# Slot sums of a mixture-of-experts layer: high and low part of an output in one product of 512 columns, four PSUM banks, halves added at the end

## The chip, the cores and the metric

The kernel runs on one core of a Trainium2 chip. The metric is the device time of one execution in microseconds; the kernel before took 657.53 us in the median of three runs (656.26 to 657.68). PE is TensorE, DVE VectorE, ACT ScalarE, POOL GpSimd and SP SyncE. PSUM, into which PE writes, has eight banks (`bank[0]` to `bank[7]`), each 512 fp32 columns on 128 partitions.

## The reference, cut to what matters

Eight sequences of 256 tokens of 256 values go through an expert layer, an attention layer and the same expert layer again:

```
x = x + 0.5 * moe(layernorm(x))
x = x + attention(layernorm(x))
x = x + 0.5 * moe(layernorm(x))

def moe(x):                      # 64 experts, 8 for each token, 32 slots for each expert, F = 96
    logits = x @ router_w.T
    wts, idx = top_k(softmax(logits), 8); wts = wts / sum(wts)
    # each expert takes its first 32 tokens, in order of position (position-major over the 8 sequences)
    h = silu(xg @ w1.T) * (xg @ v1.T)
    y = h @ w2
    return sum over the slots of a token of weight * y
```

## The kernel before, in words

An expert layer has three stages. The router computes logits, masks and, for each expert, the list of its tokens, and writes the normalised tokens to a table in HBM. Then 16 slot groups follow (`slot_step`, s = 0 to 16), each of 4 experts with 32 slots, 128 slots together. In step s PE transposes the gathered tokens of group s + 1 (L1173), adds the finished outputs of group s - 3 into the tokens (`sum_slots`, L1177), transposes `hidden` of group s - 1 (L1236), does the up products of group s (L1243) and the down products of group s - 1 (L1253). ACT copies the transposed tokens (`slotsT`, L560) and the transposed hidden values (`hiddenT`, L564), computes the gate (L570) and scales the down product to `y_parts[:, s, 0]`, the high part, rounded to fp32r (L574). DVE makes the one-hot marks (L852), the hidden values (L858) and the low part of the output (L865), which is the output less its high part. A sum product takes a one-hot matrix of 128 slots by 128 token columns as weights and `y_parts` as the moving operand, and so adds each slot's row to its token's row; high and low part are two products of 256 columns into the same place. Only the first 64 rows of each sequence (512 tokens) are summed in layer 0 (the others come into play when the last held token lies later), and 64 + 16 rows in layer 1, the 16 as "narrow" sums in `bank[5]` (L1185). The wide sums lie in `bank[6]` and `bank[7]`, each with four sequences: two on the partitions, two on the columns. Before the slots PE puts the tokens themselves there (`take_tokens`, L1212), so that the sum is the new x.

Other banks in the slot stage: `bank[0]` transposed tokens, `bank[1]` up products, `bank[2]` transposed hidden values, `bank[3]` down products, `bank[4]` slot numbers and last token. PE runs in program order, and each engine waits on semaphores; nothing but the order of the calls sets who comes first on an engine.

After layer 0 ACT copies the two banks to x in four copies (L685), DVE takes the statistics of the first tokens straight from `bank[6]` (L962), computes the moments (L806), normalises the first 512 tokens (L1040), and attention begins with nine projections (`first_fills`): two transposes xT, k, q, q, v, q, q, v. For each, ACT takes the high part out of PSUM (`take_high`) and DVE the low part (`take_low`). Between them ACT and DVE split the attention weights into high and low parts (`split_high`, `split_low`, L675 and L996); a projection waits until its weights are split (`split_by`). Weights arrive by DMA on SP's queue, the last of them `wo_raw`. `keep_busy` (L1205) gives PE products with no use in stretches where it would idle.

After layer 1 DVE copies the narrow sums to `stage` (L946), ACT `bank[6]` (L661), DVE `bank[7]` (L948), and six narrow and four wide stores go out on the queues of SP, POOL and ACT (L362, L366), each behind the semaphore `staged` of its part.

## Time and profile before

| | |
|---|---|
| median of 3 runs | 657.53 us (656.26 to 657.68) |
| profiled execution | 657.74 us, its span 655.9 us |
| layer 0's slot steps | about 38.4 to 85.4 us |
| attention | about 90.5 to 572 us |
| layer 1's slot steps | about 596.2 to 649.3 us |
| last stores issued | 652.7 us |

The span is the time from the first to the last instruction in the profile; the 1.8 us around it belong to the execution's own time. In rows of a timeline the first column is the start in us from the span's begin and the second how long the instruction, or the merged run of instructions, took. PEld rows are weight loads, which run beside the products. Ends of products on PE are modelled, so the distance between starts is the better measure. Brackets tell how long the engine was idle before the row, and for whom it waited.

### The profile page before, as it was taken

To read this page: it belongs to the slowest core of one execution; us is meant where nothing else is said; L and a number is where in the kernel's file an instruction comes from. 1 tells how busy PE (TensorE), PEld (TensorE's weight loads), DVE (VectorE), ACT (ScalarE), POOL (GpSimd) and SP (SyncE) were. 2 spreads that over 40 slices of the span, in tenths; PEclk is the share of its full clock that TensorE was granted. 3 is DMA by queue.
4 is the path that set the end of the run, shared out by engine and by line. 5 is a ranking of instruction groups with operands and counts; after the bars stand their busy time and mean duration, and the time that the engine had idled before them with its cause. 6 is when DMAs were issued, how large, how long until landed. Compare 5 with 4: busy or idle time off the path is not lost.

```text
span 655.9 us, 12187 instructions
## 1 busy us (share of the span) xinstructions
PE 623.6 (95%) x4572; PEld 536.4 (82%) x4572; DVE 504.9 (77%) x1316; ACT 386.0 (59%) x1048; POOL 52.2 (8%) x75
## 2 busy tenths in 40 slices
PE   8589989999999999999999999999999998997995
PEld 6367777999889999999889999989899997774774
DVE  6836668889997778889777788877788888694663
ACT  5724476677666655666665666656566665581442
POOL 3343000000000000000000000000000000034310
PEclk9779999999999999999999999999999999977998
DMA  8999870000000000000000000000000007175993
GB/s 315 338 412 418 307 263 1 2 1 1 0 1 1 1 1 1 0 1 1 1 1 1 1 0 1 1 1 1 1 0 1 1 11 311 36 270 182 420 397 105
DMA packets 27621, 62.53 MB, mean 95 GB/s; under 512 B 7014, under 2 KB 17382, under 8 KB 27558
## 3 DMA queue, kind: packets, MB, share of 16 engines
q1 hardware_dynamic: 25398, 55.97, 22.6%
q0 software_dynamic: 1664, 5.30, 2.1%
q8 instruction: 39, 0.64, 0.4%
q10 hardware_dynamic: 496, 0.43, 0.3%
q14 instruction: 24, 0.20, 0.1%
HBM read 54.34 MB, written 7.34 MB: 94 GB/s over the span
## 4 chain that ended last, share of the span: by engine, by line
PE 77%; DVE 10%; DMA 7%; ACT 2%; issue 1%; SPq 1%; POOL 0%; another core or an unknown queue 0%; POOLq 0%; DVEq 0%
PE bank L1401 19%; PE bank L1403 19%; PE bank L1402 19%; PE bank L1457 8%; PE bank L1243 3%; PE bank L1201 3%; DMA wo_raw<-wo_in 2%; DMA down_r<-down_in 2%; PE bank L1253 2%; PE bank L1173 1%; DMA slots<-token_table,slot_index 1%; DMA x<-x_in 1%; DVE probsT_lo L1101 1%; DVE negmax L1066 1%; DVE ln L806 1%
## 5 line engine op out<-in xcount | busy, mean ns | idle before, releaser
L718 ACT ACTIVATE probs<-bank,negmax 128x256 f32<-128x256 f32 x256 | 121.4, 494 | 0.7 <-DVE negmax L1066 0.6
L726 ACT CAST probsT_hi<-bank 128x512 fp32r<-128x512 f32 x128 | 68.7, 590 | 71.0 <-PE bank L1457 71.0
L701 ACT ACTIVATE o_hi<-bank,bv 128x512 fp32r<-128x512 f32 x64 | 44.2, 690 | 66.7 <-PE bank L1403 66.7
L1101 DVE TENSOR_TENSOR probsT_lo<-bank,probsT_hi 128x512 fp32r<-128x512 f32 x128 | 81.8, 680 | 0.5 <-ACT probsT_hi L726 0.5
L1066 DVE TENSOR_REDUCE negmax<-bank 128x2 f32<-128x512 f32 x128 | 81.7, 680 | 0.0
L1074 DVE TENSOR_SCALAR probs<-probs,rowinv 128x256 f32<-128x256 f32 x256 | 73.1, 349 | 2.3
L1401 PE MATMUL bank<-wo_hi,o_hi 128*128 128x256 f32 x256 | 73.1, 285 | 0.0
L1403 PE MATMUL bank<-wo_hi,o_lo 128*128 128x256 f32 x256 | 72.6, 284 | 0.0
L1403 PE MATMUL bank<-k_hi,q_lo 128*128 128x256 f32 x256 | 72.4, 283 | 0.0
L1402 PE MATMUL bank<-k_lo,q_hi 128*128 128x256 f32 x256 | 72.4, 283 | 0.0
L1402 PE MATMUL bank<-wo_lo,o_hi 128*128 128x256 f32 x256 | 72.3, 282 | 0.0
L1401 PE MATMUL bank<-k_hi,q_hi 128*128 128x256 f32 x256 | 72.2, 282 | 0.0
L1052 DVE SCALAR_TENSOR_TENSOR o_lo<-bank,bv,o_hi 128x512 fp32r<-128x512 f32 x64 | 48.0, 750 | 28.7 <-ACT o_hi L701 28.7
L1052 DVE SCALAR_TENSOR_TENSOR q_lo<-bank,bq,q_hi 128x512 fp32r<-128x512 f32 x64 | 47.9, 748 | 25.5 <-ACT q_hi L701 25.3
L1457 PE MATMUL bank<-ident,probs 128*128 128x128 f32 x512 | 66.4, 273 | 0.7 <-DVE probs L1074 0.7
L1457 PEld LDWEIGHTS bank<-ident,probs 128*128 128x128 f32 x512 | 57.3, 140 | 1.1 <-DVE probs L1074 1.1
L718 ACT ACTIVATION_READ_ACCUMULATOR probs<-bank,negmax 128x1 f32 x256 | 57.7, 226 | 0.0
L1401 PE MATMUL bank<-xT_hi,wq_hi 128*128 128x512 f32 x128 | 54.4, 425 | 1.0 <-DVE k_lo L1052 1.0
L1401 PE MATMUL bank<-probsT_hi,v_hi 128*128 128x512 f32 x128 | 51.1, 399 | 3.1 <-DVE probsT_lo L1101 2.9
L701 ACT ACTIVATE q_hi<-bank,bq 128x512 fp32r<-128x512 f32 x64 | 45.0, 703 | 12.5 <-PE bank L1403 12.5
L1401 PEld LDWEIGHTS bank<-k_hi,q_hi 128*128 128x128 f32 x256 | 48.8, 191 | 2.8 <-DVE q_lo L1052 0.3
L1402 PEld LDWEIGHTS bank<-k_lo,q_hi 128*128 128x128 f32 x256 | 48.8, 191 | 2.4
(181 smaller groups left out, 1342.7 us busy)
## 6 DMA issues: line engine op xcount, KB each, us to landing
up_r<-up_in SPq DMA_DIRECT2D x16, 768.0 KB
down_r<-down_in SPq DMA_DIRECT2D x14, 512.0 KB
up_q<-up_in SPq DMA_DIRECT2D x8, 768.0 KB, 8.8
up_o<-up_in SPq DMA_DIRECT2D x6, 768.0 KB
down_q<-down_in SPq DMA_DIRECT2D x8, 512.0 KB, 9.6
token_table<-xn SPq DMA_DIRECT2D x16, 256.0 KB, 2.4
down_o<-down_in SPq DMA_DIRECT2D x6, 512.0 KB
x<-x_in SPq DMA_DIRECT2D x4, 512.0 KB, 5.6
```

What stands on the lines that cost most here:

```text
L701: nc.scalar.activation(dst, src, ACT.Identity, bias=bias).then_inc(work_high, 1)
L718: nc.scalar.activation(probs[:, n % 2, t, :], scores_ps[head][:, qt * S:qt * S + S], ACT.Exp, bias=negmax[:, n % 2, t:t + 1], accum_out=ro ...
L726: nc.scalar.copy(probsT[0][:, head].rearrange("p c s -> p (c s)"), probsT_ps[head][:]).then_inc(probsT_high, 1)
L1052: nc.vector.scalar_tensor_tensor(lo, src, bias, hi.bitcast(f32), ALU.add, ALU.subtract).then_inc(work_taken, 1)
L1066: nc.vector.reduce_max(negmax[:, n % 2, 2 * head:2 * head + 2], scores_ps[head][:].rearrange("p (t s) -> p t s", t=2), AX.X, negate=True). ...
L1074: last = nc.vector.tensor_scalar(probs[:, n % 2, t, :], probs[:, n % 2, t, :], rowinv[:, n % 2, t:t + 1], None, ALU.mult)
L1101: nc.vector.tensor_tensor(probsT[1][:, head].rearrange("p c s -> p (c s)"), probsT_ps[head][:], probsT[0][:, head].rearrange("p c s -> p ( ...
L1201: last = mm(banks[n][:, D * pair:D * pair + D], marks[:, c:c + P], parts, start=start and pair == 0, stop=stop, skip_group_check=True)
L1401: mm(dst, w[0], m[0], start=start, stop=False, skip_group_check=shared)
L1402: mm(dst, w[0], m[1], start=False, stop=False, skip_group_check=shared)
L1403: return mm(dst, w[1], m[0], start=False, stop=stop, skip_group_check=shared)
L1457: last = nc.tensor.transpose(probsT_ps[head][:, c * S + qt * P:c * S + qt * P + P], probs[:, n % 2, 2 * head + qt, c * P:c * P + P], ident[:])
```

## The change

`sum_slots` issues one product of 512 columns where it issued two of 256: the moving operand is high and low part side by side. The high sums come to the first 256 columns of a bank and the low sums to the last 256. A bank then holds two sequences and not four, so that the wide sums take four banks (`wide_ps` = banks 2, 3, 6, 7), and the narrow ones all 512 columns of bank 5. The tokens go into the high halves, with `start=True` (banks 2 and 3 last, after the logits in them were copied). At the end ACT copies the high half to `stage` and DVE adds the low half to it, for each of the four banks and for the narrow one; the result goes to x after layer 0 and stays in `stage` after layer 1.

The banks freed for this: transposed hidden values move from bank 2 to free columns of bank 0, down products from bank 3 to bank 4. PE therefore waits for ACT's copy of the transposed tokens before it transposes `hidden`, and in step 1 for `limit_ready` before the down products. After layer 0 one `finish_tokens` stands ahead of the statistics, which are now taken from x, one behind the normalisation, and two behind the first two fills. The splits of weights on ACT are placed anew among the fills, and `keep_busy` after layer 0's sums has 16 products for 20.

```diff
-        def wide_sums(banks, b):
-            return banks[b // 4][WIDE * (b % 2):WIDE * (b % 2) + WIDE, D * (b // 2 % 2):D * (b // 2 % 2) + D]
+        wide_ps, narrow_ps, down_ps, idle_ps = bank[2:4] + bank[6:8], bank[5], bank[4], bank[1]
+        def pair_rows(b, low=0):
+            return wide_ps[b // 2][WIDE * (b % 2):WIDE * (b % 2) + WIDE, D * low:D * low + D]
...
-        def rows_of_bank(n, odd, count=4):
-            first = 4 * n + odd
-            return x[0:WIDE, 2 * first:2 * (first + count - 1):4, :]
+        narrow_stage = stage[:, 2, 0:D]
+        def stage_of(n):
+            return stage[:, n // 2, D * (n % 2):D * (n % 2) + D]
...
                     nc.scalar.copy(hiddenT[:],
-                                   bank[2][0:F, 0:P]).then_inc(hiddenT_ready, 1)
+                                   bank[0][0:F, KD * P:KD * P + P]).then_inc(hiddenT_ready, 1)
                 if layer == 0 and s == GROUPS:
...
                     act.wait_ge(down_done, down_seen.add())
-                    nc.scalar.activation(y_parts[:, s - 1, 0, :], bank[3][:, 0:D],
+                    nc.scalar.activation(y_parts[:, s - 1, 0, :], down_ps[:, 0:D],
                                          ACT.Identity, scale=slot_weight[:, s - 1:s]).then_inc(y_high, 1)
...
                 if layer == 1:
-                    act.wait_ge(bank_summed, 2 + 2)
-                    nc.scalar.copy(stage[:, 0, :], bank[6][:]).then_inc(staged[0], 1)
-                    act.wait_ge(staged[0], 1)
+                    copy_high_sums(PAIRS, narrow_stage, narrow_ps)
+                    for n in range(PAIRS):
+                        copy_high_sums(PAIRS + 1 + n, stage_of(n), wide_ps[n])
+                    act.wait_ge(staged[0], 2)
                     for odd in range(2):
                         store_wide(nc.scalar, 0, odd)
-                    act.wait_ge(staged[1], 1)
+                    act.wait_ge(staged[1], 2)
                     store_wide(nc.scalar, 1, 1)
...
+            def copy_high_sums(seen, dst, sums):
+                act.wait_ge(bank_summed, seen + 1)
+                nc.scalar.copy(dst, sums[:, 0:D]).then_inc(high_copied, 1)
             def split_high(n):
...
             expert_layer(0)
-            for n in range(2, 5):
+            for n in range(2, 4):
                 split_high(n)
             act.wait_ge(small_loaded, 64)
-            for n, seen in ((1, (bank_summed, 2)), (0, (first_sums_read, 1))):
-                act.wait_ge(*seen)
-                for odd in range(2):
-                    nc.scalar.copy(rows_of_bank(n, odd), bank[6 + n][WIDE * odd:WIDE * odd + WIDE, :].rearrange(
-                        "p (b d) -> p b d", b=2)).then_inc(x_final, 1)
-            split_high(5)
+            for n in range(PAIRS):
+                copy_high_sums(n, stage_of(n), wide_ps[n])
+            for n in range(4, 6):
+                split_high(n)
...
             warm(ACT.Exp)
-            for n in range(6, 8):
-                split_high(n)
             act.wait_ge(bq_scaled, 1)
             for n, job in enumerate(first_fills):
+                if n == 5:
+                    act.wait_ge(x_final, PAIRS)
                 take_fill(*job)
-                if 1 <= n < 5:
-                    split_high(n + 7)
+                if 1 <= n < 6:
+                    split_high(n + 5)
+                if n == len(first_fills) - 1:
+                    split_high(11)
                 if n >= SCORES_AT and n < SCORES_AT + 2:
...
                 else:
-                    dve.wait_ge(bank_summed, 2 + 1)
-                    nc.vector.tensor_copy(stage[:, 2, 0:D], bank[5][:, 0:D]).then_inc(staged[2], 1)
-                    dve.wait_ge(bank_summed, 2 + 3)
-                    nc.vector.tensor_copy(stage[:, 1, :], bank[7][:]).then_inc(staged[1], 1)
+                    add_low_sums(PAIRS, narrow_stage, narrow_ps, staged[2])
+                    for n in range(PAIRS):
+                        add_low_sums(PAIRS + 1 + n, stage_of(n), wide_ps[n], staged[n // 2])
...
                 with nc.vector.If(most >= FIRST[layer]):
-                    dve.wait_ge(bank_summed, (2, 5)[layer])
+                    dve.wait_ge(bank_summed, (PAIRS, 2 * PAIRS + 1)[layer])
                     for r in range(1, RANGES):
...
-                    last.then_inc(first_sums_read, 1)
-                    dve.wait_ge(first_sums_read, 1)
+                        last = nc.vector.bn_stats(stats[0:WIDE, 2 * odd, :], x[0:WIDE, 2 * odd, :])
+                    tie(last)
+            def add_low_sums(seen, dst, sums, done):
+                dve.wait_ge(high_copied, seen + 1)
+                nc.vector.tensor_tensor(dst, dst, sums[:, D:2 * D], ALU.add).then_inc(done, 1)
+            def finish_tokens(n):
+                dve.wait_ge(high_copied, n + 1)
+                for odd in range(2):
+                    rows = slice(WIDE * odd, WIDE * odd + WIDE)
+                    last = nc.vector.tensor_tensor(x[0:WIDE, 2 * (2 * n + odd), :], stage_of(n)[rows, :], wide_ps[n][rows, D:2 * D], ALU.add)
+                last.then_inc(x_final, 1)
...
             dve.wait_ge(bo_ready, 1)
-            dve.wait_ge(x_final, 4)
             normalise_tokens(0)
+            finish_tokens(1)
             for n, job in enumerate(first_fills):
...
                     normalise_probs(0)
+                if n < 2:
+                    finish_tokens(n + 2)
                 for m in in_fill.get(n, []):
                     split_low(m)
+            dve.wait_ge(x_final, PAIRS)
             step(0)
...
                 marks = onehot[:, s % MARKS, :]
+                parts = y_parts[:, s, :, :].rearrange("p l d -> p (l d)")
                 if layer == 1:
-                    for low in range(2):
-                        last = mm(bank[5][:, 0:D], marks[:, RANGE:FIRST[1]], y_parts[:, s, low, :], start=False,
-                                  stop=final and low == 1, skip_group_check=True)
+                    last = mm(narrow_ps[:], marks[:, RANGE:FIRST[1]], parts, start=False, stop=final, skip_group_check=True)
                     if final:
                         last.then_inc(bank_summed, 1)
-                for n in range(2):
-                    for low in range(2):
-                        last = sum_wide(bank[6:8], n, marks, y_parts[:, s, low, :], False, final and low == 1)
+                for n in range(PAIRS):
+                    last = mm(wide_ps[n][:], marks[:, n * P:n * P + P], parts, start=False, stop=final, skip_group_check=True)
                     if final:
...
-            def take_tokens():
-                for b in range(B):
-                    mm(wide_sums(bank[6:8], b), ident[:, 0:WIDE], x[:, 2 * b, :], start=b % 4 < 2, stop=False,
+            def take_tokens(layer):
+                for b in (4, 5, 6, 7, 0, 1, 2, 3):
+                    if b == 0:
+                        pe.wait_ge(logits_ready, 4 * layer + 4)
+                    mm(pair_rows(b), ident[:, 0:WIDE], x[:, 2 * b, :], start=True, stop=False,
                        skip_group_check=True, tile_position=(0, WIDE * (b % 2)))
...
                 for b in range(B):
-                    mm(bank[5][:, 0:D], rows_into_place(b), x[WIDE:WIDE + NARROW, 2 * b, :], start=b == 0, stop=False,
+                    mm(narrow_ps[:, 0:D], rows_into_place(b), x[WIDE:WIDE + NARROW, 2 * b, :], start=b == 0, stop=False,
                        skip_group_check=True)
...
                 if s > 0:
+                    if s + 1 < GROUPS:
+                        pe.wait_ge(slotsT_ready, sT_seen.now() + 1)
                     pe.wait_ge(hidden_ready, hidden_seen.add())
-                    nc.tensor.transpose(bank[2][0:F, 0:P], hidden[:],
+                    nc.tensor.transpose(bank[0][0:F, KD * P:KD * P + P], hidden[:],
                                         ident[:]).then_inc(hiddenT_raw, 1)
...
                     pe.wait_ge(down_free, free_seen.add())
+                    if s == 1:
+                        pe.wait_ge(limit_ready, layer + 1)
                     for j in range(EG):
-                        last = mm(bank[3][32 * j:32 * j + 32, 0:D],
+                        last = mm(down_ps[32 * j:32 * j + 32, 0:D],
                                   hiddenT[:, 32 * j:32 * j + 32],
...
                 if layer == 0:
-                    keep_busy(20)
+                    keep_busy(16)
                 pe.wait_ge(limit_ready, layer + 1)
...
                 project(*job)
+            pe.wait_ge(x_final, PAIRS)
             step(0)
-            pe.wait_ge(x_final, 4)
             for i in range(BLOCKS - 1):
```

## Rows read from the trace of the kernel before

**Rows 1.** Page, part 1: busy us (share of the span) xinstructions of each engine.
```profile
PE 623.6 (95%) x4572; PEld 536.4 (82%) x4572; DVE 504.9 (77%) x1316; ACT 386.0 (59%) x1048; POOL 52.2 (8%) x75
```

**Rows 2.** Timeline, one slot step of layer 0: start, duration, engine, line, operands.
```profile
62.57 0.44 PE L1173 MATMUL bank<-ident,slots 128*128 128x128 f32 x2
...
62.74 1.01 PEld L1201 LDWEIGHTS bank<-y_parts,onehot 128*128 128x128 f32 x8
...
62.77 0.47 ACT L574 ACTIVATE y_parts<-bank,slot_weight 128x256 fp32r<-128x256 f32 x1 [0.24 <-PE bank L1253]
...
63.14 0.36 ACT L560 COPY slotsT<-bank 128x256 f32<-128x256 f32 x1
...
63.69 0.12 PEld L1236 LDWEIGHTS bank<-ident,hidden 128*96 128x96 f32 x1
...
65.22 0.44 PE L1173 MATMUL bank<-ident,slots 128*128 128x128 f32 x2
```

**Rows 3.** Timeline, the same point in two steps of layer 1.
```profile
629.87 0.44 PE L1173 MATMUL bank<-ident,slots 128*128 128x128 f32 x2
...
632.75 0.44 PE L1173 MATMUL bank<-ident,slots 128*128 128x128 f32 x2
```

**Rows 4.** Timeline, a projection: first and last of five 512-column products in a row.
```profile
97.02 0.39 PE L1402 MATMUL bank<-xT_lo,wq_hi 128*128 128x512 f32 x1
...
97.94 0.40 PE L1403 MATMUL bank<-xT_hi,wq_lo 128*128 128x512 f32 x1
```

**Rows 5.** Timeline, steps 1 and 2 of layer 0's slots.
```profile
42.90 0.15 PEld L1236 LDWEIGHTS bank<-ident,hidden 128*96 128x96 f32 x1 [0.33 <-DVE hidden L858]
...
43.01 0.37 ACT L560 COPY slotsT<-bank 128x256 f32<-128x256 f32 x1 [0.45 <-PE bank L1173]
...
44.94 0.12 PEld L1236 LDWEIGHTS bank<-ident,hidden 128*96 128x96 f32 x1
...
45.23 0.36 ACT L560 COPY slotsT<-bank 128x256 f32<-128x256 f32 x1
```

**Rows 6.** Timeline, steps 1 and 2 of layer 1's slots.
```profile
601.03 0.15 PEld L1236 LDWEIGHTS bank<-ident,hidden 128*96 128x96 f32 x1 [1.29 <-DVE hidden L858]
...
601.85 0.37 ACT L560 COPY slotsT<-bank 128x256 f32<-128x256 f32 x1 [1.16 <-remote]
...
603.97 0.20 PEld L1236 LDWEIGHTS bank<-ident,hidden 128*96 128x96 f32 x1
...
604.42 0.37 ACT L560 COPY slotsT<-bank 128x256 f32<-128x256 f32 x1
```

**Rows 7.** Windows: length, PE, PEld, DVE, ACT, POOL busy, granted clock, DMA share, GB/s.
```profile
600.00:602.00 2.00, 0.97 (x9) 0.55 (x13) 1.14 (x7) 0.41 (x2) 0.89 (x1) 0.50 0.54 107
```

**Rows 8.** Timeline, from the last sums of layer 0 into attention.
```profile
85.20 0.87 DVE L962 BATCH_NORM_STATS2 stats<-bank 64x6 f32<-64x256 f32 x2 [0.17 <-PE bank L1201]
...
85.36 4.55 PEld L1209 LDWEIGHTS bank<-router_w,ident 128*128 128x128 f32 x40
...
88.52 1.38 DVE L1040 TENSOR_SCALAR xn<-x,ln 128x256 f32<-128x256 f32 x4
...
90.50 0.86 PEld L1424 LDWEIGHTS bank<-ident,xn 128*128 128x128 f32 x8 [0.59 <-DVE xn L1040]
...
91.86 1.29 DVE L1050 TENSOR_TENSOR xT_lo<-bank,xT_hi 128x512 fp32r<-128x512 f32 x2 [1.96 <-ACT xT_hi L699]
...
94.64 0.63 ACT L675 ACTIVATE wo_hi<-wo_raw 128x512 fp32r<-128x512 f32 x1 [2.32 <-DMA wo_raw<-wo_in]
...
97.81 0.68 DVE L996 SCALAR_TENSOR_TENSOR wv_lo<-wv_raw,wv_hi 128x512 fp32r<-128x512 f32 x1
```

**Rows 9.** Timeline, the end of the kernel.
```profile
648.37 0.42 DVE L946 COPY stage<-bank 128x256 f32<-128x256 f32 x1 [0.65 <-PE bank L1185]
...
649.28 0.69 DVE L948 COPY stage<-bank 128x512 f32<-128x512 f32 x1 [0.48 <-PE bank L1201]
...
649.44 2.08 ACTq L362 DMA_DIRECT2D out<-stage  x3
```

More of the change, by code:

```diff
@@ L865, in slot_step @@
                     nc.vector.scalar_tensor_tensor(
[L866 removed]
+                        y_parts[:, s - 1, 1, :], down_ps[:, 0:D], slot_weight[:, s - 1:s],
                         y_parts[:, s - 1, 0, :].bitcast(f32), ALU.mult, ALU.subtract).then_inc(down_free, 1)
@@ L1317, in expert_layer @@
                 if layer == 1:
-                    take_tokens()
+                    take_tokens(layer)
                 pe.wait_ge(code_ready, PARTS * (layer + 1))
@@ L1335, in expert_layer @@
                 if layer == 0:
-                    take_tokens()
+                    take_tokens(layer)
                 else:
```

12 lines of the change are left out of this document (6 added, 6 removed).

## The prediction, made before the kernel was run

> **What bounds the kernel now.** I read the page's busy shares first: PE is busy for 95% of the span, DVE for 77%, ACT for 59% [rows 1]. A product saved on PE can therefore pay, but only where PE is the one that the step waits for. So I went to the timeline of the slot steps, the only place where the sums stand. In layer 0 a step takes 2.65 us (65.22 - 62.57), and between these starts PE does not rest: eight sum products, then the transposed `hidden`, the up and the down products [rows 2]. In layer 1, with two narrow products more, it takes 2.88 us (632.75 - 629.87) [rows 3]. PE alone sets these steps. Then I read, in order of time, the three places that the change touches besides: the first two steps of each layer, the passage from layer 0 to attention, and the last stores.
>
> **The sum products.** In rows 2 the eight sums begin at 62.74 and the next weight load stands at 63.69: 0.95 us, or 0.118 us for each 256 columns. The difference of the two steps says the same: 2.88 - 2.65 = 0.23 us for two products, 0.115 each [rows 2, 3]. What a 512-column product takes shows in a projection: five starts between 97.02 and 97.94, 0.23 us each [rows 4]. Four of them take 0.92 us where eight of 256 took 0.94 to 0.95. I take 0.02 us saved in a step of layer 0 and 0.025 us in one of layer 1 (five for ten). The bounds are 0 (by the difference of the steps, 2 x 0.115 against 0.23) and 0.05. A layer has about 15 sums that PE is waited for: 15 x 0.02 = 0.3 us and 15 x 0.025 = 0.4 us, 0.7 us for both. The number of products is halved, the number of columns is not, and columns are what PE is paid in.
>
> The Trainium skill (TensorE: Matmul & The Clock Gate, Back-to-back issue gap) gives two figures for this. Its gap for one product is N / 2.4 ns and 2.5 ns; by it four products fewer would save 0.01 us in a step. It also gives 131 ns for a 512-column product in a stream of loads and products; by that the sums of a step would fall to about 0.52 us. The trace speaks against the second: 0.23 us in just such a stream [rows 4]; I keep it as a rival's companion below.
>
> **The wait before `hidden` is transposed.** It now writes the bank from which ACT copies the transposed tokens, and PE waits for this copy. Behind the waiting transpose stand the up and down products and all that follows on PE. In a full step the copy ends at 63.14 + 0.36 = 63.50 and the transpose's load begins at 63.69, with the sums between them [rows 2]. Shorter sums take 0.03 us off this room of 0.19 us: nothing lost, and little room left. In steps 1 and 2 there are no sums to cover it. Layer 0: the copy ends at 43.38, the transpose began at 42.90, 0.48 us lost; in step 2 the copy ends at 45.59 against 44.94, 0.65 us, and since the copy there comes behind the first down product on ACT, it moves with the first loss and both add up: 1.13 us [rows 5]. PE has no rest afterwards to give them back. Layer 1: 602.22 against 601.03 is 1.19 us in step 1, and 604.79 against 603.97 is 0.82 us in step 2 [rows 6]. PE's granted clock is 0.50 there, its lower level of 1.2 GHz [rows 7]. What is pushed later runs in part after the clock is back at 2.4 GHz, so I count 1.2 us of the 2.0. Bounds: layer 0 0.5 to 1.2, layer 1 0.6 to 2.0. The wait for `limit_ready` in step 1 costs nothing: DVE has it done while PE is at the up products. In `take_tokens` the wait for the last logits has four products of banks 6 and 7 ahead of it, and I take nothing.
>
> **From layer 0 into attention.** Before: statistics from 85.20, moments, normalisation from 88.52 to 89.90 on DVE, then eight transposes on PE from 90.50, which had to wait until the 20 idle products (loads 85.36 to 89.91) and the reading of the limit were through [rows 8]. After: the first bank is complete one product (0.23 us) after its start and not four (0.47 us), 0.24 us earlier; then ACT's copy of 256 columns, 0.36 us as in rows 2, two DVE additions, and the statistics. No row shows such an addition on 64 partitions from PSUM. The nearest is the copy of 256 columns at 0.42 us [rows 9]; two one behind the other I take at 0.78 us, between 0.7 and 0.9. With a little for the semaphores the statistics begin 0.95 us later, and the normalisation ends at 90.85. The idle products, four fewer at 4.55 / 20 = 0.23 us, end 0.9 us earlier, and PE takes the transposes as the tokens come: the first xT is ready at 91.0, as before. ACT was not free before 91.2 either. Up to here nothing is lost.
>
> Then two pairs of additions (2 x 0.78 us) stand in DVE's queue behind xT's low parts, ahead of the weight splits. One more pair falls in the 1.96 us in which DVE was idle before 91.86 [rows 8]. Against them stands a gain: ACT's high part of k no longer waits behind a split for which `wo_raw` landed only at 94.64. Taken in order with the durations of before (low part and split 0.68 us each, a projection 1.38 us): xT's second low part ends at 93.9, split 3 at 95.3, k's low part at 96.4, split 4 at 97.0, q's low part at 98.4, split 5 at 99.0. In the profile of before this last one, `wv_lo`, ended at 98.49, and v's projection followed it. So 0.5 us are lost; the bounds are -0.6 (the two pairs find room, and k's earlier high part counts) and 1.6 (neither finds any). Attention behind it is PE's, and passes a delay on.
>
> **The end.** Before, `bank[7]` was in `stage` at 649.97 (649.28 + 0.69), and ACT began its stores at 649.44 [rows 9]. Now ACT has five copies of about 0.35 us one after the other from 648.37, and DVE an addition behind each, at 0.42 us. The first two banks are ready at about 649.95 and the last at 650.6. ACT's three stores take 2.08 us on its queue and begin at 650.0, 0.55 us later than before; the last bank is ready before the third of them. So 0.55 us, between 0.2 and 0.8.
>
> **Sum.** -0.3 + 1.13 + 0.5 in layer 0 and behind it, -0.4 + 1.2 in layer 1, +0.55 at the end: 2.7 us. On the profiled execution's 657.74 us this gives 660.4; it stood 0.2 us above the median of 657.53 us, so I forecast 660.2 us.
>
> **Rivals.** (A) The products of 512 columns are cheaper in this stream than in the projection, because only half as many weight loads stand between them. It is on the other side: from 0.1 us saved in each of some 30 steps the 2.7 us and the 0.7 us already counted are paid (3.4 / 30 = 0.11), and at 0.2 us a step the kernel would take 660.2 + 0.7 - 6 = 654.9 us. For it speaks that a load of 128 columns is itself 0.19 us long. Against it speaks that in rows 4 loads and products stand in the same alternation, and that 0.23 us is already close to what 512 columns need at 2.4 GHz (0.213 us). By the skill's 131 ns, named above, it would be the case at its far end. 8 in 100.
>
> (B) The waits and additions find cover: the clock gives back most of what steps 1 and 2 lose, and k's early high part pays for the additions. Then 0.5 + 0.6 - 0.3 - 0.7 + 0.55 leaves 0.6 us: 658.2 us. For it speaks DVE's idle time in the first fills, against it that DVE and PE follow each other there with little room. 18 in 100.
>
> (C) The new gaps keep PE's clock low for longer. It was down to 0.50 in layer 1 [rows 7], where PE's loads had stood idle for 1.29 us [rows 6], and the change adds gaps of 0.5 to 1.2 us in both layers and takes idle products away ahead of attention. A step of 2.88 us at half the clock takes up to 2.9 us more; one such stretch gives 662 to 663 us. The skill (TensorE: Matmul & The Clock Gate, HAM oscillation) warns only of long idleness; by it these gaps would change nothing. The trace has the lower clock beside a gap of about a microsecond, so I give it 14 in 100.
>
> **How the numbers follow.** The forecast has 60 in 100, with a range of its own from 658.7 to 661.8 us. The range for 8 in 10 reaches into B and C: 657.5 to 663.0 us. A change within 0.2% (1.3 us, what a measurement of this kernel tells from none) comes from most of B and the lower edge of the forecast: 0.19. Faster by more is A and a little of B: 0.10. Slower 0.71.
>
> **What would show it.** Right: a slot step of 2.62 to 2.65 us in layer 0 and about 2.86 in layer 1, with sum products 0.23 us apart; the loads of L1236's transpose in steps 1 and 2 right behind ACT's copy of `slotsT`, with PE idle before them for about 0.5 to 1.2 us; split 5 (`wv_lo`) later than before, reckoned from the last sum; the stores of ACT half a microsecond further from the last sum. Wrong: steps of 2.55 us or less (A); v's projection no later from the last sum than before (B); a granted clock of 0.5 beyond step 3 or in the first fills (C); or a full step in which the transpose of `hidden` waits for the copy, which the 0.19 us of room exclude in my reckoning and which would cost up to 0.1 us in each of 26 steps.

## The result, and the profile after

The changed kernel takes 662.18 us (median of 9 runs, 660.24 to 664.94); the kernel before took 658.78 us beside it (9 runs, 656.26 to 660.23). The ratio is 1.0042, with a 95% interval of 1.0022 to 1.0062: slower by 0.4%. The profiled execution took 660.75 us, with a span of 658.7 us against 655.9 us before. The forecast was 660.2 us, in a range from 657.5 to 663.0 us. Two single executions far outside all others, 969.74 us in after_fill20 and 2709.69 us of the kernel before beside before_order_fill16, are in no ratio and no median below.

The total hides several differences of both signs. I cut both traces at the same events (us, from the start of one event to the start of the next). "Keys" is PE's transpose of the slot keys, the end of the router's work, and the first of them started at 31.15 us before and at 30.99 us after:

```
stage                                              before   after   diff
first keys of layer 0 -> last sums of layer 0       53.28   52.69  -0.59
last sums of layer 0 -> v's projection              14.18   18.89  +4.71
v's projection -> keys of layer 1 (attention)      493.87  493.96  +0.09
keys -> first transposed slots of layer 1            3.76    6.39  +2.63
first transposed slots -> last sums of layer 1      51.60   48.40  -3.20
last sums -> ACT's stores                            1.60    2.06  +0.46
ACT's stores -> end                                  6.49    5.27  -1.22
```

The page's busy shares answer to [rows 1]: 152 products fewer on PE (144 of the sums, 8 of the idle ones), and only 3.4 us less of busy time.

```profile
PE 620.2 (94%) x4420; PEld 527.5 (80%) x4420; DVE 509.2 (77%) x1327; ACT 386.5 (59%) x1052; POOL 52.4 (8%) x75
```

One full slot step of layer 0 (timeline: start, duration, engine, line, operands), answering [rows 2]. The sums are four loads of L1213 where there were eight. The step is 50.89 - 48.26 = 2.63 us long.

```profile
48.26 0.44 PE L1197 MATMUL bank<-ident,slots 128*128 128x128 f32 x2
...
48.43 0.76 PEld L1213 LDWEIGHTS bank<-y_parts,onehot 128*128 128x128 f32 x4
...
48.83 0.37 ACT L565 COPY slotsT<-bank 128x256 f32<-128x256 f32 x1
...
49.25 0.12 PEld L1262 LDWEIGHTS bank<-ident,hidden 128*96 128x96 f32 x1
...
50.89 0.44 PE L1197 MATMUL bank<-ident,slots 128*128 128x128 f32 x2
```

The same point in layer 1, answering [rows 3]: 2.86 us.

```profile
613.46 0.44 PE L1197 MATMUL bank<-ident,slots 128*128 128x128 f32 x2
...
616.32 0.44 PE L1197 MATMUL bank<-ident,slots 128*128 128x128 f32 x2
```

Steps 1 and 2 of layer 0, answering [rows 5]. The bracket behind a row is the engine's idle time before it and what ended it: `hidden`'s transpose now comes behind ACT's copy of `slotsT` and nothing else.

```profile
41.28 0.37 ACT L565 COPY slotsT<-bank 128x256 f32<-128x256 f32 x1 [0.23 <-PE bank L1197]
...
41.71 0.12 PEld L1262 LDWEIGHTS bank<-ident,hidden 128*96 128x96 f32 x1 [0.70 <-ACT slotsT L565]
...
43.75 0.36 ACT L565 COPY slotsT<-bank 128x256 f32<-128x256 f32 x1
...
44.16 0.12 PEld L1262 LDWEIGHTS bank<-ident,hidden 128*96 128x96 f32 x1 [0.79 <-ACT slotsT L565]
```

The same steps in layer 1, answering [rows 6].

```profile
606.67 0.12 PEld L1262 LDWEIGHTS bank<-ident,hidden 128*96 128x96 f32 x1 [1.39 <-ACT slotsT L565]
...
609.13 0.12 PEld L1262 LDWEIGHTS bank<-ident,hidden 128*96 128x96 f32 x1 [0.79 <-ACT slotsT L565]
```

The passage into attention, answering [rows 8]. The copies and additions are there, and the last tokens' `xn` are ready at 88.94 + 1.38 = 90.32. But PE, after three of the eight transposes, loads nothing from 90.19 to 93.76, and the trace names no releaser ("issue").

```profile
84.42 1.17 ACT L679 COPY stage<-bank 128x256 f32<-128x256 f32 x4
...
84.80 0.85 DVE L984 TENSOR_TENSOR x<-stage,bank 64x256 f32<-64x256 f32 x2
...
88.94 1.38 DVE L1061 TENSOR_SCALAR xn<-x,ln 128x256 f32<-128x256 f32 x4
...
90.05 0.14 PEld L1452 LDWEIGHTS bank<-ident,xn 128*128 128x128 f32 x1 [0.19 <-DVE xn L1061]
...
93.76 0.93 PEld L1452 LDWEIGHTS bank<-ident,xn 128*128 128x128 f32 x5 [3.57 <-issue]
...
94.33 0.59 ACT L707 CAST xT_hi<-bank 128x512 fp32r<-128x512 f32 x1 [6.18 <-PE bank L1452]
...
101.78 0.68 DVE L1017 SCALAR_TENSOR_TENSOR wv_lo<-wv_raw,wv_hi 128x512 fp32r<-128x512 f32 x1
...
102.58 0.19 PEld L1429 LDWEIGHTS bank<-wv_hi,xT_hi 128*128 128x128 f32 x1 [1.29 <-DVE q_lo L1073]
```

The chain of waits (start, duration, what) has the same stretch as time in which the engine waited for nothing that the profile shows:

```profile
90.38 3.38 issue
```

Windows (length; busy time of PE, PEld, DVE, ACT, POOL with instruction counts; granted clock, DMA share, GB/s) show that all compute engines rest together while the DMA engines still move the weights, and that PE then works at half the clock:

```profile
90.00:92.00 2.00, 0.38 (x2) 0.14 (x1) 1.16 (x3) 0.00 (x0) 0.00 (x0) 1.00 1.10 389
92.00:94.00 2.00, 0.24 (x1) 0.24 (x2) 0.00 (x0) 0.00 (x0) 0.00 (x0) 0.91 0.65 225
94.00:96.00 2.00, 2.00 (x11) 2.00 (x11) 1.04 (x3) 1.46 (x3) 0.00 (x0) 0.50 0.03 10
```

The DMA queues from 90 to 94 us (packets, MB, share of the time of 16 engines): the bulk transfers of q1, and a single packet of q8, whose kind is "instruction". It has 16,384 bytes, began at 91.45 and took 0.96 us.

```profile
q1 hardware_dynamic: 1198, 1.21, 86.1%
q8 instruction: 1, 0.02, 1.5%
```

The end, answering [rows 9]: five copies on ACT, five additions on DVE, and ACT's stores 2.06 us after the last sums' first load (651.33), where it was 1.60. ACTq rows are the issuing of stores.

```profile
651.33 0.19 PEld L1209 LDWEIGHTS bank<-y_parts,onehot 128*128 128x128 f32 x1 [0.31 <-issue]
...
651.87 1.48 ACT L679 COPY stage<-bank 128x256 f32<-128x256 f32 x5 [1.17 <-PE bank L1209]
652.28 1.75 DVE L977 TENSOR_TENSOR stage<-stage,bank 128x256 f32<-128x256 f32 x5 [1.06 <-ACT stage L679]
...
653.39 2.04 ACTq L367 DMA_DIRECT2D out<-stage  x3
```

The span closes 0.45 us after the last of the stores has landed, before and after. That is ACT's last narrow store, issued at 652.25 before and at 656.12 after. In the view of DMA issues its last number is the time to landing; before, then after:

```profile
out<-stage ACTq DMA_DIRECT2D x1, 16.0 KB, 3.2
```

```profile
out<-stage ACTq DMA_DIRECT2D x1, 16.0 KB, 2.1
```

One more row matters below: PE's compare-and-branch behind a layer's sums, which runs twice. Its three numbers are the shortest, the median and the longest duration in ns, then the two starts. Before, then after:

```profile
L1360 PEldq COMPARE_BRANCH  x2: 1642/2502/3361, 88.8 to 648.6; - x2
```

```profile
L1388 PEldq COMPARE_BRANCH  x2: 367/388/409, 87.2 to 652.0; - x2
```

### The profile page after: what moved, and what is told of

Read it like the earlier page. It is cut to its first block, busy times and chain, and to the rows that moved or that the text cites. A ratio compares the mean times of both kernels' runs of the same rounds, so it can differ in the third digit from the quotient of the medians.

```text
span 658.7 us, 11926 instructions
## 1 busy us (share of the span) xinstructions
PE 620.2 (94%) x4420; PEld 527.5 (80%) x4420; DVE 509.2 (77%) x1327; ACT 386.5 (59%) x1052; POOL 52.4 (8%) x75
## 3 DMA queue, kind: packets, MB, share of 16 engines
HBM read 54.34 MB, written 7.34 MB: 94 GB/s over the span
## 4 chain that ended last, share of the span: by engine, by line
PE 78%; DVE 11%; DMA 5%; ACT 3%; issue 1%; SPq 0%; POOL 0%; POOLq 0%; DVEq 0%; ACTq 0%
PE bank L1429 20%; PE bank L1431 19%; PE bank L1430 19%; PE bank L1485 8%; PE bank L1213 3%; PE bank L1269 3%; DMA down_r<-down_in 2%; PE bank L1281 2%; DVE ln L816 1%; PE bank L1197 1%; DMA x<-x_in 1%; DVE probsT_lo L1122 1%; DVE negmax L1087 1%; PE bank L1231 1%; DMA slots<-token_table,slot_index 1%
```

## The experiments

Ratios are to the kernel before, run beside each kernel, with 95% intervals. "After" is the changed kernel.

**after_again**: the changed kernel once more, without an edit.

> The changed kernel once more, to see whether the stop of PE between the third and the fourth token transpose ahead of attention (3.4 us, with all four tokens ready) comes again. Theory F (PE's instructions arrive late: their fetch queues behind the weights' DMA traffic, and with fewer idle products PE comes to the missing block earlier): the stop is there again, over 2 us long, and ends when the weight traffic ends. Theory N (a chance event of one execution): it is gone, and from the last sums of layer 0 to v's projection it takes about 15 us where the one profile had 18.9. The time is 1.004 of before's either way by the nine runs.

660.27 us (9 runs; before 657.67), ratio 1.0047 [1.0030, 1.0065]; span 658.3. The stop in the transposes is there again (waits: engine, waited for, us in total, times, longest):

```profile
PEld bank L1452 <- issue: 3.2, 1, 3.2
```

From the last sums to v's projection it took 18.37 us. So the stop belongs to the program, not to one execution.

**after_fill20**: as many idle products ahead of attention as before.

```
-                    keep_busy(16)
+                    keep_busy(20)
```

> The changed kernel with 20 idle products after layer 0's sums, as before the change, in place of 16. Theory F: PE asks for the next block of code at the same place of its program but has 0.9 us more of work queued; if the stop is a matter of how much work covers the fetch, it shrinks by 0.9 us and no more time is lost elsewhere: within 1 us of the changed kernel, faster if anything. Theory P (my prediction's step: the idle products only hold PE up, DVE sets the transposes): the same time, or up to 0.5 us slower, as the last transposes wait for the idle products.

662.77 us (5 runs), ratio 1.0091 [1.0066, 1.0116]; span 660.2. Fewer fillers were not the harm; four more cost a further 2.5 us over after_again. PE's stop grew and moved into the branch, which began at 89.30 and ended at 95.39 us:

```profile
L1388 PEldq COMPARE_BRANCH  x2: 3325/4706/6086, 89.3 to 652.7; - x2
```

```profile
95.44 1.57 PEld L1452 LDWEIGHTS bank<-ident,xn 128*128 128x128 f32 x8 [5.05 <-issue]
```

**after_wo_late**: `wo`'s raw weights are loaded only when the last layer-0 work is released, so that less traffic runs in the passage.

```
             sp.wait_ge(down_done, done_with_o)
+            sp.wait_ge(work_ready, 1)
```

> The changed kernel with the 2 MB load of wo_raw issued only after PE has transposed the first half of the tokens, so that no weight traffic runs while PE crosses from layer 0 into attention. Theory F: the stop of 3.4 us goes (PE resumes within 0.3 us of the fourth token), PE's clock does not fall behind it, and the kernel is 3 to 5 us faster than the changed one, about 0.997 of before. Theory P (DVE's additions and splits set this stretch, DMA traffic does not matter): no difference, or slower by up to 1 us where ACT waits for wo_raw before its ninth split.

658.66 us (12 runs), ratio 1.0017 [0.9998, 1.0036]; span 654.6. The stop has shrunk from 3.4 to 0.5 us: the fourth transpose comes at 90.96, its `xn` was ready at 90.44 (the bracket in its row names DVE, but DVE was done by then). The branch takes 371 ns. From the last sums to v's projection it took 15.73 us, 3.16 less than in after.

```profile
90.16 0.14 PEld L1453 LDWEIGHTS bank<-ident,xn 128*128 128x128 f32 x1 [0.19 <-DVE xn L1062]
90.96 0.53 PEld L1453 LDWEIGHTS bank<-ident,xn 128*128 128x128 f32 x5 [0.66 <-DVE xn L1062]
```

**before_wo_late**: the same edit on the kernel before.

> The kernel before with the same later load of wo_raw. There PE had no stop in this stretch, but ACT waited until 94.64 us for wo_raw, and the high part of k behind it. Theory F: there is little to gain, as the fetch was in time; what remains is ACT's wait: 0 to 1.5 us faster or slower, since wo_raw lands later than before and ACT's ninth split stands ahead of the high part of k: 0.998 to 1.003. If the traffic costs in other ways too, it gains as much as the changed kernel does.

662.15 us (6 runs), ratio 1.0074 [1.0048, 1.0100]; span 659.2. This run tells nothing on the branch: in the old order ACT's split of `wo` stands ahead of k's high part, and now waits for the later load. PE then rests for 5.42 us and works at half the clock behind it.

```profile
99.15 0.63 ACT L676 ACTIVATE wo_hi<-wo_raw 128x512 fp32r<-128x512 f32 x1 [6.28 <-DMA wo_raw<-wo_in]
...
101.19 0.29 PEld L1402 LDWEIGHTS bank<-xT_hi,wq_hi 128*128 128x128 f32 x1 [5.42 <-DVE k_lo L1053]
```

**after_split256**: every 512-column sum becomes two of 256 columns into the halves of its bank; the waits, the copies and additions stay. For the four wide banks (the first bank alike):

```
-  last = mm(wide_ps[n][:], marks[...], parts, start=False, ...)
+  for low in range(2):
+      last = mm(wide_ps[n][:, D * low:D * low + D], marks[...],
+                parts[:, D * low:D * low + D], start=False, ...)
```

> The changed kernel with every sum product taken apart again: two products of 256 columns, high and low part, into the two halves of the same bank. Two questions. Price of a product: by my prediction a slot step of layer 0 takes 2.65 us as before the change and 0.02 to 0.03 us more than with 512 columns, so 0.7 us more in all; by rival A it would be 0.1 us or more a step. Place of the code: PE has as many instructions ahead of the branch after layer 0's sums as before the change, apart from the 28 or so new waits. Theory F says that the 3.4 us stop hangs on where the blocks of PE's code begin: it moves or goes. If the stop stays between the third and the fourth token transpose, theory F's account of its place is wrong.

664.37 us (6 runs; before 658.94), ratio 1.0076 [1.0048, 1.0103]; span 663.2. A full step takes 2.65 us in layer 0 and 2.88 in layer 1, as before the change. So the wide products are worth 0.02 us a step. The kernel is slower than after by more than that: its trace shows half the clock from 83.1 to 86.5 and from 605.3 to 615.5 us, and over its six timed runs the mean granted clock was 0.970, against 0.977 for the kernel before beside it. It also has no stop in the transposes (its branch takes 1.95 us, the passage 15.55 us).

**late_hidden5**: after_wo_late, and in layer 0 `hidden` is transposed into bank 5, so that the new wait stands only in layer 1.

```
+def hidden_place(layer):
+    return bank[5][0:F, 0:P] if layer == 0 else bank[0][0:F, KD * P:KD * P + P]
-                    if s + 1 < GROUPS:
+                    if s + 1 < GROUPS and layer == 1:
                         pe.wait_ge(slotsT_ready, sT_seen.now() + 1)
```

> The changed kernel with wo_raw loaded later (so that the stop of PE is out of the way), and in layer 0 the transposed hidden values in bank 5, which is idle there, so that PE need not wait for the copy of the transposed tokens; layer 1 as changed. My prediction's step (the wait costs where no sums cover it): steps 1 and 2 of layer 0 lose their gaps of about 0.5 us each, and the slots of layer 0 get 0.9 to 1.1 us shorter against the kernel with the late wo_raw alone, at the same clock; nothing changes from step 3 on. Rival B (the clock and other waits cover them): no difference over 0.3 us.

660.29 us (12 runs), ratio 1.0013 [0.9998, 1.0029]; span 658.9. Steps 1 and 2 of layer 0 take 2.02 and 1.91 us, against 2.37 and 2.46 in after: the wait costs 0.35 + 0.55 = 0.9 us there. The whole stage of layer 0 is no shorter, though (52.77 against 52.69 us), and the ratio hardly moves against after_wo_late's 1.0017: 0.9 us is less than the intervals can tell. In these rows `hidden` is transposed without a wait for the copy:

```profile
41.31 0.12 PEld L1265 LDWEIGHTS bank<-ident,hidden 128*96 128x96 f32 x1 [0.35 <-DVE hidden L871]
...
43.07 0.12 PEld L1265 LDWEIGHTS bank<-ident,hidden 128*96 128x96 f32 x1
```

**before_late_order**: the kernel before, with the late load and with ACT's splits of the weights moved so that `wo`'s stands behind k's high part.

```
+            sp.wait_ge(work_ready, 1)
-                if 1 <= n < 5:
-                    split_high(n + 7)
+                if 4 <= n < 8:
+                    split_high(n + 4)
```

> The kernel before with wo_raw loaded later and ACT's splits of it moved behind the fills of k and the first two of q, so that the high part of k waits for no transfer. PE's program is unchanged. If the wait for wo_raw cost the kernel before anything, this is faster: k's high part about 1 us earlier, 0.5 to 1.5 us in all (0.998). If DVE sets the stretch, no difference.

659.79 us (12 runs), ratio 1.0006 [0.9990, 1.0022]; span 656.1. It is the partner of after_wo_late: 1.0006 against 1.0017. The new order alone gives 0.9979 (before_order, below), so the late load may cost something, and after_wo_late may understate what the stop costs; the two were not measured beside each other, and their orders differ by one place. In the passage the trace shows no such cost: 13.57 us from the last sums to v's projection, 13.72 in before_order.

**before_wait**: the kernel before, with the wait of the change alone.

```
+                    if s + 1 < GROUPS:
+                        pe.wait_ge(slotsT_ready, sT_seen.now() + 1)
```

> The kernel before with only the new wait of PE for the copy of the transposed tokens ahead of the transpose of hidden, in both layers. My prediction: 1.1 us lost in layer 0's steps 1 and 2, 1.2 in layer 1's, nothing from step 3 on: 2.3 us, 1.0035. Rival B: 1.0 us or less. The added instructions also move PE's code by some 30 places; by theory F that alone may cost or give back up to several us between the layers, which the profile would show as a stop of PE at or behind the branch.

663.35 us (12 runs), ratio 1.0056 [1.0036, 1.0075]; span 662.0. By itself the wait costs no less than the whole change (1.0042 and 1.0047), and more than the 1.0035 expected. It made PE rest at the first steps, and the clock stayed at its lower level over further steps: 3.93, 3.82 and 3.07 us for steps 1 to 3 of layer 0, and 5.53, 3.82 and 3.81 us in layer 1. This was not the profiled execution alone: over the twelve timed runs the mean granted clock was 0.969, against 0.977 for the kernel before beside them.

```profile
40.00:44.00 4.00, 3.10 (x26) 1.49 (x30) 1.22 (x8) 1.02 (x4) 0.91 (x1) 0.59 1.02 421
44.00:48.00 4.00, 3.54 (x31) 1.50 (x33) 1.72 (x8) 1.54 (x5) 0.95 (x1) 0.50 1.02 422
48.00:52.00 4.00, 4.00 (x39) 2.62 (x35) 2.00 (x10) 1.21 (x5) 0.95 (x1) 0.63 1.01 418
```

The kernel before without this wait has the full clock from 44 us on; its row of the same stretch:

```profile
44.00:48.00 4.00, 4.00 (x57) 2.37 (x49) 3.13 (x13) 2.13 (x7) 1.57 (x2) 1.00 1.02 422
```

**after_pad4**: four more idle products at the very start of the kernel's products, far from the passage. They move PE's later code by four products, as after_fill20 does, and leave the queued work of the passage as in after.

```
-            for _ in range(5):
+            for _ in range(9):
```

> The changed kernel, 16 idle products as there, with four more idle products at the very start of the kernel (9 for 5), where PE waits for the first data anyway. This puts PE's code behind them at the place that it has in the kernel with 20 idle products after layer 0's sums, without the work queued there. Theory F (the place of the code decides): the branch behind the sums, 0.37 us in the changed kernel and 6.1 us in the one with 20, now takes several us, the stop in front of the fourth token is gone or moved, and the time lies with that kernel's (1.009) and not with the changed kernel's (1.0045). Theory Q (the queued work decides): branch and stop as in the changed kernel, and its time.

664.81 us (6 runs; before 659.78), ratio 1.0085 [1.0063, 1.0108]; span 660.7. The passage shows after_fill20's picture, not after's:

```profile
84.38 3.76 PEld L1231 LDWEIGHTS bank<-router_w,ident 128*128 128x128 f32 x32
...
93.82 1.57 PEld L1452 LDWEIGHTS bank<-ident,xn 128*128 128x128 f32 x8 [5.68 <-issue]
```

```profile
L1388 PEldq COMPARE_BRANCH  x2: 3780/5252/6725, 87.0 to 652.7; - x2
```

So with the work queued as in after, a shift of the code alone moved the stop into the branch and brought after_fill20's time.

**late_best**: late_hidden5, with the last two tokens' additions moved behind fills 2 and 3, and in steps 1 and 2 of layer 1 the up products ahead of `hidden`'s transpose.

```
-                if n < 2:
-                    finish_tokens(n + 2)
+                if 2 <= n < 4:
+                    finish_tokens(n)
+                up_first = layer == 1 and s in (1, 2)
+                for part in (("up", "hidden") if up_first else ("hidden", "up")):
```

> The changed kernel with the late wo_raw, hidden values in bank 5 in layer 0, and two steps more: DVE's last two pairs of additions stand behind the third and fourth fill, where it waited for ACT, and in steps 1 and 2 of layer 1 the up products come ahead of the transpose that waits. Against the kernel with only the first two: v's projection 0.5 to 0.8 us nearer to the last sum of layer 0 (if the additions held xT's low part and split 3 up), and steps 1 and 2 of layer 1 0.4 to 0.8 us shorter together at full clock. In all 657 to 658 where before has 657.5 to 659: 0.998 to 1.000. If the additions were covered, the first term is 0.

659.18 us (12 runs), ratio 1.0009 [0.9989, 1.0030]; span 656.3. Nothing is gained that the measurement can tell: from the eighth transpose of `xn` to v's projection it took 8.42 us, against 8.30 with the additions where the change has them, and steps 1 and 2 of layer 1 took 3.50 and 2.39 us. The moved additions were not out of the way: the last of them stands right ahead of the split on which v's projection (99.74) waits.

```profile
98.07 0.84 DVE L987 TENSOR_TENSOR x<-stage,bank 64x256 f32<-64x256 f32 x2
...
98.94 0.69 DVE L1020 SCALAR_TENSOR_TENSOR wv_lo<-wv_raw,wv_hi 128x512 fp32r<-128x512 f32 x1
```

**before_order**: the kernel before, with only ACT's splits moved.

```
-                if 1 <= n < 5:
-                    split_high(n + 7)
+                if 3 <= n < 7:
+                    split_high(n + 5)
```

> The kernel before with only ACT's splits moved: the two of wo_raw that stood behind the second and third fill stand behind the fourth and fifth, the others follow. Loads and PE's program are unchanged. In the profile of before ACT waited until 94.64 for wo_raw with k's high part queued behind. If that wait set v's projection, it comes about 1 us nearer to the last sum, and the kernel is 0.5 to 1.2 us faster (0.998 to 0.999); if DVE's chain sets it, as my prediction had it for the changed kernel, nothing changes.

658.03 us (12 runs; before 659.78), ratio 0.9979 [0.9967, 0.9992]; span 657.1. Faster than the kernel before by 0.2%. k's high part no longer waits behind `wo`'s split, and v's projection comes 13.72 us after the last sums, 0.46 sooner than before:

```profile
95.10 0.75 DVE L1052 SCALAR_TENSOR_TENSOR k_lo<-bank,bk,k_hi 128x512 fp32r<-128x512 f32 x1 [1.29 <-ACT k_hi L701]
...
96.35 0.62 ACT L675 ACTIVATE wo_hi<-wo_raw 128x512 fp32r<-128x512 f32 x1
...
97.95 0.19 PEld L1401 LDWEIGHTS bank<-wv_hi,xT_hi 128*128 128x128 f32 x1 [0.82 <-DVE q_lo L1052]
```

**before_order_fill16**: before_order with `keep_busy(16)` for `keep_busy(20)`.

> The kernel before with ACT's splits moved as in the run that was faster than both, and 16 idle products for 20 after layer 0's sums. By the work alone: the idle products kept PE from the tokens until 90.50, and DVE had all four by 89.95, so up to 0.5 us more is won, 0.9975 of before. Theory F warns: PE's code behind them moves by 16 instructions, and the branch, 1.5 us and covered by the queued idle products, may take several us under the weights' traffic; then it is slower than the kernel with 20, by up to 4 us (1.002 to 1.005), and the profile shows a long branch or a stop behind it.

656.37 us (12 runs; before 657.86), ratio 0.9981 [0.9965, 0.9998]; span 652.1. Fewer fillers add nothing to the gain of the order (0.9979). Here the branch takes 2.59 us in the passage, to 89.43, and the first transpose comes right behind it, 0.5 us after all `xn` were ready (88.93); no stop is in the transposes:

```profile
L1360 PEldq COMPARE_BRANCH  x2: 2587/3002/3417, 86.8 to 644.7; - x2
```

```profile
89.48 0.86 PEld L1424 LDWEIGHTS bank<-ident,xn 128*128 128x128 f32 x8 [1.53 <-DVE xn L1040]
```

## Why the prediction was right, and where it was not

The direction and the total were right: +2.7 us forecast; measured +2.8 between the profiled spans, and +0.42% of the time, or 2.8 us with an interval from 1.4 to 4.1 (3.4 between the medians). The terms were not all right, and the total owes something to parts that I left out and that cancel. That part is luck.

**The sum products: right.** 0.02 us a step, measured 2.65 to 2.63 and 2.88 to 2.86. Rival A is ruled out by after_split256, and with it, for these products, the Trainium skill's 131 ns for 512 columns (TensorE: Matmul & The Clock Gate, Back-to-back issue gap): in this stream it is 0.23 us.

**The waits in steps 1 and 2: right in place, somewhat oversized.** Forecast 1.13 us in layer 0, measured 0.9 against late_hidden5. Forecast 1.2 in layer 1. There steps 1 and 2 together, in all traces with the full clock in them, took 4.82 to 5.56 us with the wait (after, after_again, after_fill20, after_pad4, after_wo_late; mean 5.1) and 3.68 to 4.75 without (before_wo_late, before_order_fill16, before_late_order; mean 4.2): 0.9 us. Step 1 varies because it follows a gather. What a step loses also did not reach the stage's length in layer 0 between after_wo_late and late_hidden5: other waits vary by as much.

**The passage: the step that failed.** I wrote that PE "takes the transposes as the tokens come: the first xT is ready at 91.0, as before". ACT could take it only at 94.33. I had 0.5 us with an upper bound of 1.6; the stage lost 4.7. late_hidden5, which has no stop, splits this. Without the stop the passage takes 15.26 us against 14.18, 1.1 us more: the eighth transpose comes 0.2 us later from the last sums, and v's projection 0.9 us later from there, where I had 0 and 0.5. So the additions were mis-sized by a factor of two, within the bound. The other 3.6 us are the stop (3.4) and the transposes behind it at half the clock, which took 0.3 us longer. after_wo_late (15.73 us) still holds 0.5 us of the stop. By the timed runs, side by side on the same chip, the late load moves the ratio from 1.0047 to 1.0017, 2.0 us; the two intervals overlap a little. That the additions make the whole of the 1.1 is not shown: late_best moved two pairs of them, but to places where v's projection still waited for them.

What the stop is: PE, ACT and DVE idle from 91.2 us on, all data ready, no semaphore awaited. It shrank when the weights' traffic was moved (after_wo_late), and it moved with the position of PE's code, with the same work queued (after_pad4). The reading that fits both is that PE's next block of code arrives late under the bulk transfers. The traces say more than that. Each of the 16 KB packets of kind "instruction" on q8 has a start and a duration, and PE goes on at a fixed distance behind one (us):

```
                             packet        packet's end -> PE goes on
after, 4th transpose         91.45 0.96    92.41 -> 93.76   1.35
after_again, 4th transpose   91.75 0.96    92.71 -> 93.99   1.28
after_wo_late, 4th transp.   88.55 1.16    89.71 -> 90.96   1.25
after_fill20, branch's end   93.05 0.95    94.00 -> 95.39   1.39
after_pad4, branch's end     91.44 0.95    92.39 -> 93.76   1.37
before, branch's end         88.02 0.90    88.93 -> 90.44   1.51
```

The same holds for all 18 branches of 1 us or more in the fourteen traces: each ends 1.35 to 1.56 us after such a packet ended. In front of the ten branches of 0.32 to 0.41 us the last such packet had ended 6.4 us or more before they began. So a branch's length is set here by when the packet comes: before the branch in the kernel before (88.02 against 88.80), 3.75 us after its start in after_fill20 and 4.40 us in after_pad4, both amid the weights' traffic, and 1.0 us after its start at the end of both kernels, where the weights' traffic is long past (3.33 and 3.78 us in all). That the packet carries the code for which PE waits is still inferred, from this regularity; no run could take the fetch away alone. Why the packet comes so much later in some kernels is open. The Trainium skill (Advanced Engine Details and Errata, ISA Cache) gives a cache line of 16 KB, for 256 instructions, and says that there are only two. The size is that of these packets; the number of lines no run here shows.

**The end: the term 0.55 was 0.46, and the sign of the whole was wrong.** The stores began later as said, but the kernel ended 1.2 us sooner behind them. From the last sums to the end it took 8.10 us before, 7.34 and 7.28 in after and after_again, 8.26 in after_fill20 and 8.61 in after_split256. The end hangs on the landing of ACT's last store. It was issued 4.4 us after the last sums before and 4.8 after, as the later copies want it, but landed in 2.1 us and not in 3.2. This goes with PE's second branch and with the place of the code: in the five kernels with a short one (0.32 to 0.41 us) the last store landed in 2.0 to 2.2 us, in the nine with a long one (2.4 us or more) in 3.0 to 3.6. The branch itself is not on the path, it ends 3.9 us or more before the kernel does. In those nine a 16 KB instruction packet starts within 1.0 us behind the issue of that store (653.22 behind 652.25 in before), in the five none does. So the code's position, which cost 3 us in the passage, gave back about 1 at the end; that the packet delays the store is inferred. I had looked at neither.

**The clock.** Rival C's mechanism is real: before_wait shows it, in both layers. It did not decide in after's slot steps, which had the full clock; nor, on the average, in the timed runs: the mean granted clock was 0.977 in after_again, 0.978 in after_wo_late and 0.978 in the kernel before beside them. (In the nine runs of the first measurement it was 0.974 for the changed kernel; of the kernel before beside it only the profiled execution's clock is on record, 0.973.) But it hides the waits in the table. In layer 1 the profile of before had the lower clock during its steps [rows 7], with 4.16 + 3.13 us for steps 1 and 2, while after had it during its idle products before the first slots. Those two account for most of the -3.20 and +2.63 us. With the full clock in the steps, the old order's stage takes 47.22, 47.86 and 48.05 us (before_order_fill16, before_late_order, before_wo_late), the new one's 47.73 to 49.36 in five traces, 0.9 us more in the mean, where I had 1.2 - 0.4 = 0.8. In layer 0, too, before had half the clock in steps 1 and 2 (40.2 to 43.6 us) and after did not. From the first transposed slots to the last sums it took 46.05 before and 46.02 after; with the full clock the old order takes 45.44 and 45.49 (before_order_fill16, before_late_order), 0.6 us less, where I had 1.1 - 0.3 = 0.8. Nearly all of the table's -0.59 lies ahead of the first slots. These are phases of single executions, and the change didn't bring them: before_late_order, with the old sums, also took 6.71 us from keys to slots.

**Sum.** Piece by piece, from traces at the full clock and without the stop, the forecast's terms are -0.3 + 0.9 + 1.1 in layer 0 and behind it, -0.4 + 0.9 in layer 1, +0.5 at the end: 2.7 us, as forecast, with waits too large and additions too small by about the same. The timed runs can't confirm this so closely. after_wo_late gave 1.0017 [0.9998, 1.0036], 1.1 us. In this the faster end is contained (5.41 us behind the first of ACT's stores, where before had 6.49), and 0.5 us of the stop; with +1.1 and -0.5 for them it comes to about 1.7 us, with some 1.2 us of uncertainty: below my 2.7, and rival B's 0.6 is not excluded. In after's profile the stop (+3.6) and the end (-1.2) come on top, which would give 5.1 us, and the clock phases and the waits for gathers of the two executions take about 2.4 off. So the total was hit with a middle part about right and large parts missing that mostly cancel.

## What to carry to other kernels

A change in the number of instructions moves all the code behind it. Where an engine's stream crosses a branch or a long stretch of new code while bulk DMA traffic runs, look at the traces for "issue" idle time with all data ready and for a DMA packet of kind "instruction" that ended shortly before it does, and compare kernels of different length before a few microseconds are put down to the edit; a pad of idle instructions elsewhere tells the two apart. Merging products of the same columns saved 0.02 us for four; the bank that the merged output took from others cost more. And before rebuilding the sums, look for a queue order such as ACT's split that waits on a DMA ahead of work that is ready: moving it gave 0.2%, which the rebuilt sums did not.

## What was not expected of the hardware

- One compare-and-branch of PE took from 0.32 to 6.7 us, depending on the kernel's length and on the place. The Trainium skill (Advanced Engine Details and Errata, Control Flow Timing) gives about 108 ns; PE's was that short in no run here.
- The long ones end 1.35 to 1.56 us after a 16 KB packet of kind "instruction" has ended, all 18 of them.
- The same last store of 16 KB landed in 2.0 to 2.2 us in five kernels and in 3.0 to 3.6 us in nine, according to whether such a packet came behind its issue.
- With a wait added in two steps (0.86 us each in layer 0), the granted clock stayed at 0.50 for about 10 us in each layer (40.7 to 50.9 and 603.9 to 614.1 us in before_wait), where the kernel before had 3.4 us (40.2 to 43.6) and 6.8 us (600.0 to 606.8). In after, with the same wait, layer 0 had the full clock there. In layer 1 two of the seven traces of the changed kernel with this wait had such a stretch too (late_hidden5 601.9 to 612.1, after_split256 605.3 to 615.5 us). What decides is open.
